# The two attention passes of a vision tower: a new order of score units, a running ring of banks, and folded tiles

## The chip, the cores and the metric

The kernel runs on one core of a Trainium2 chip. The metric is device time in microseconds for one launch, lower is better. Trace times are microseconds from the start of the profiled execution.

## The reference, cut to what matters

64 images become 197 tokens of 192 channels each (a patch embedding, plus a class token). Then attention with 12 heads of 16 channels, in which every operand is fake-quantised to 8 bits with ONE scale per whole tensor, and a mixture of experts with a layernorm. What matters here:

```python
q, k, v = (qkv[0], qkv[1], qkv[2])
attn = jnp.einsum('bhnd,bhmd->bhnm', fake_quant(q), fake_quant(k)) * scale
attn = jax.nn.softmax(attn, axis=-1)
out = jnp.einsum('bhnm,bhmd->bhnd', fake_quant(attn), fake_quant(v))
out = jnp.einsum('bnc,oc->bno', fake_quant(out), fake_quant(w_proj)) + b_proj
```

The scale of `attn` is the maximum over all images and heads, so the softmax has to be known in whole before it can be quantised: the scores are made twice.

## The kernel before, in words

Images are worked in couples, 32 of them. **The first pass** (`attend_maxima`, from L687) makes, for each couple, the integer q and k (two matmuls per group of 4 heads, three groups, into `pqk`; DVE multiplies and rounds into `qkv_y`, L962; POOL takes the magic number off into `qk_int`, L754), the integer v (two full tiles, a tile with tokens 128 to 191 of both images, a tile with the last five tokens), and all scores. SP copies k from the odd rows of `qk_int` to `k_int` (four DMAs, L727, once all three groups are integers) and saves q, k and v to HBM.

The scores of a couple are 37 tiles of 128 partitions x 197: 24 with tokens 0 to 127, 12 with tokens 128 to 191 of both images folded on 128 partitions, and one with the last five tokens of all heads and both images. They are worked in 10 **units**: u0 to u5 are 4 whole tiles each, u6 and u7 are 4 folded tiles each, u8 is 2 folded tiles, u9 is 2 folded tiles and the last tile (the last tile is six matmuls over `q_ends`, L896, each with 128 columns of weights, one after the other in the same accumulation). A unit goes through four engines: PE makes the scores into one of three PSUM tiles `s0..s2` (L881, L889), DVE takes each row's maximum (L976, L970), POOL multiplies it by minus alpha (L810, L808), and ACT makes exp(alpha*s - alpha*max) tile by tile with the row's sum accumulated (L939). PE may use a PSUM tile again when ACT is through with the unit that had it. The order within a couple is u0 to u9; the PSUM tile is u mod 3, but u9 has tile 1:

```python
def bank_of(u):
    return 1 if u == UNITS - 1 else u % 3
def before(u):
    return (6, 9, 8, 0, 1, 2, 3, 4, 5, 7)[u]
```

So u9 waits for the exps of u7, and u1 of the next couple for those of u9. Between the units each engine does a share of the next couple's q, k, v: POOL's copies of token ends after u0, integers after u2, u3 and u4 (`integers`), `q_ends` and the first value tiles after u5, the second value tile after u7 (`values_second`, L787: four instructions whose two scalars are columns in SBUF, all 128 partitions each, with a mask for the image), the last after u9 (`values_last`). All engines run their programs in order; `need_apart` is a wait and a small increment on the same engine.

**Between the passes** (`attend`, from L992) the shifts log(sum)/alpha - max are split into three bfloat16 parts: DVE does the columns of the whole tiles (L1107 to L1111), POOL those of the folded tiles and of the last tile (L1053 to L1062), for the first 4 couples and then for the 28 others. In between them POOL runs `partition_all_reduce` (L1066) for the smallest sum. PE transposes the parts, DVE and ACT copy them out, and DMAs lay them into rows of q in HBM, which k meets with ones.

**The second pass** (`attend`, second half) reloads q, k, v from HBM by SP, makes the scores transposed with the shift in them, in the same units and the same order, with three PSUM tiles `st0..st2`. ACT makes the exps of a whole unit at once (L1320) into one of three SBUF tiles `exps` (`bank_of` again). DVE (units 0, 2, 4, 6, 8, 9) or POOL (1, 3, 5, 7) rounds to bfloat16 integers (L1171). After the scores of u5 PE makes the products of the couple before: 60 matmuls of 198 columns (L1276, L1285). DVE takes them out (`outputs`, L1340, L1341: two instructions for each image's channels 0 to 127 and two for each image's channels 128 to 191, the latter on 64 partitions) and takes each couple's peaks (L1349) after u9. SP's order is q, k and v of one couple, then of the next.

## Time and profile before

| | us |
|---|---|
| median of 3 runs | 2516.96 (2514.52 to 2522.5) |
| the profiled execution | 2516.79 |
| its span, first to last instruction | 2515.0 |
| start of the span to 503 (embedding, norm, scales) | 503 |
| first pass, 503 to 1119 | 616 |
| between the passes, 1119 to 1150 | 31 |
| second pass, 1150 to 1490 | 340 |
| the rest (projection, gate, experts, norm) | 1025 |

How to read it: the busy share of an engine over the whole span says little, since the stages differ. The attention passes repeat one couple 32 times, so that a microsecond in a couple's period is 32 us in the end. "idle ... <-" in a row is the time in which the engine stood still just before, and who released it. PE, DVE, ACT and POOL are TensorE, VectorE, ScalarE and GpSimd, PEld is TensorE's weight load, SPq is the queue on which SyncE issues DMAs.

### The profile page before, as it was taken

What the parts mean: (1) busy time and instruction counts of PE and PEld (TensorE: products, weight loads), DVE (VectorE), ACT (ScalarE), POOL (GpSimd) and SP (SyncE); (2) the same over time, 40 slices, a digit from 0 to 9 for tenths busy, and PEclk for the clock granted to TensorE, in tenths of its full rate; (3) what the DMA queues carried; (4) which work ended last, traced back from release to release, by engine and by line L of the source; (5) the groups of instructions that cost most, each with busy time, mean ns of one, the idle gap of its engine ahead of it and who ended that gap; (6) DMA issues with size and microseconds to landing.
All of it is one profiled execution on the core that took longest, in us unless ns stands there. A gap on an engine that the chain in (4) does not pass through costs nothing. (4 is left out here: it accounts for less than half of the span.)

```text
span 2515.0 us, 51890 instructions
## 1 busy us (share of the span) xinstructions
PE 1568.9 (62%) x12385; PEld 1067.6 (42%) x12386; DVE 1549.1 (62%) x4019; ACT 1298.6 (52%) x3763; POOL 1260.0 (50%) x1953
## 2 busy tenths in 40 slices
PE   2999938645555555534666636666614788876464
PEld 2999934311111111112334323433304667665453
DVE  0555569956666666653666657777746555553797
ACT  0222215358888888875777743333312444443454
POOL 2333300066666666643333323776754566655588
PEclk9999968955555555555666555555557998998787
DMA  5344200011112112114333333333313333332675
GB/s 169 152 164 181 117 30 1 1 61 71 67 61 72 67 60 72 67 42 101 112 107 105 105 100 105 126 124 118 108 59 87 107 101 105 107 106 58 198 244 179
DMA packets 180866, 252.50 MB, mean 100 GB/s; under 512 B 27664, under 2 KB 143839, under 8 KB 177092
## 3 DMA queue, kind: packets, MB, share of 16 engines
q1 hardware_dynamic: 132196, 189.10, 23.9%
q0 software_dynamic: 20704, 40.98, 4.7%
q10 hardware_dynamic: 27888, 21.50, 2.7%
q8 instruction: 34, 0.56, 0.1%
q14 instruction: 44, 0.36, 0.0%
HBM read 140.66 MB, written 107.86 MB: 99 GB/s over the span
## 5 line engine op out<-in xcount | busy, mean ns | idle before, releaser
L939 ACT ACTIVATE exps_summed<-s,neg_shift 128x197 f32<-128x197 f32 x1184 | 484.9, 449 | 118.5 <-POOL neg_shift L810 115.7
L976 DVE TENSOR_REDUCE score_max<-s 128x788 f32 (+3 forms) x320 | 279.9, 891 | 89.5 <-PE s L881 61.8
L2032 POOL DMA_INDIRECT expert_sums<-y_tile,row_places x216 | 215.6, 998 | 165.5 <-ACT y_tile L2132 98.2
L1320 ACT ACTIVATE exps<-st,scalars 128x788 f32<-128x788 f32 (+1 forms) x320 | 256.6, 867 | 71.9 <-DVE probs L1171 30.0
L939 ACT ACTIVATION_READ_ACCUMULATOR exps_summed<-s,neg_shift (+1 forms) x1184 | 270.9, 229 | 0.0
L351 PE MATMUL mm<-w_tok,x_transposed 128*112 128x192 f32 x1344 | 238.7, 328 | 0.0
L351 PEld LDWEIGHTS mm<-w_tok,x_transposed 128*112 128x112 f32 x1344 | 214.5, 178 | 0.1
L1171 POOL TENSOR_SCALAR probs<-exps 128x788 bf16<-128x788 f32 x128 | 108.9, 851 | 197.0 <-ACT exps L1320 196.3
L296 ACT COPY x_transposed<-tp 128x672 f32<-128x672 f32 x112 | 80.6, 719 | 240.9 <-PE tp L342 240.9
L328 POOL TENSOR_SCALAR x_patches<-x_tile 112x768 f32<-112x768 f32 x112 | 93.1, 832 | 223.3 <-PE tp L342 181.7
L1171 DVE TENSOR_SCALAR probs<-exps 128x788 bf16<-128x788 f32 (+1 forms) x192 | 115.3, 614 | 117.8 <-ACT exps L1320 114.0
L889 PE MATMUL s<-k_int,qk_int 16*64 16x197 bf16 x768 | 59.6, 369 | 177.7 <-ACT exps_summed L939 177.7
L881 PE MATMUL s<-k_int,qk_int 16*128 16x197 bf16 x768 | 97.7, 355 | 110.3 <-ACT exps_summed L939 106.2
L382 DVE TENSOR_TENSOR h_rows_all<-mm,posb 112x192 f32<-112x192 f32 (+1 forms) x112 | 40.1, 358 | 178.3 <-PE mm L351 125.7
L962 DVE TENSOR_SCALAR qkv_y<-pqk,scalars 128x394 f32<-128x394 f32 (+1 forms) x192 | 116.9, 609 | 33.9 <-PE pqk L857 20.3
L1560 POOL DMA_INDIRECT listed_rows<-z_rows_a,row_index x99 | 101.4, 1024 | 70.1 <-issue 36.3
L754 POOL TENSOR_SCALAR qk_int<-qkv_y,scalars 128x394 bf16<-128x394 f32 x96 | 122.5, 1276 | 17.4 <-DVE qkv_y L962 10.1
L2125 ACT ACTIVATE g<-dn,down_bias 128x256 f32<-128x256 f32 x216 | 93.1, 494 | 70.6 <-remote 43.3
L810 POOL TENSOR_TENSOR neg_shift<-score_max,neg_alpha 128x4 f32<-128x4 f32 (+1 forms) x320 | 64.0, 200 | 119.6 <-DVE score_max L976 119.4
L2266 PE MATMUL weighted<-sum_a,weight_diagonals 128*128 128x192 f32 (+1 forms) x198 | 65.8, 423 | 84.7 <-DVE weight_diagonals L2322 60.1
L2089 PE MATMUL up<-up_hi,g_hi 128*128 x432 | 112.1, 260 | 7.7 <-issue 4.2
L2158 DVE TENSOR_TENSOR z_lo<-zt,z_hi 128x256 f16<-128x256 f32 x108 | 45.2, 419 | 116.4 <-ACT z_hi L2118 90.8
(411 smaller groups left out, 4714.1 us busy)
## 6 DMA issues: line engine op xcount, KB each, us to landing
x_tile<-in_x SPq DMA_DIRECT2D x24, 1568.0 KB
z_tile<-listed_rows SPq DMA_DIRECT2D x108, 196.0 KB
v_ints<-v_slots SPq DMA_DIRECT2D x32, 480.0 KB, 2.5
v_slots_in<-v_ints SPq DMA_DIRECT2D x32, 480.0 KB, 3.3
q_ints<-qk_int SPq DMA_DIRECT2D x32, 295.5 KB, 2.5
k_ints<-k_int SPq DMA_DIRECT2D x32, 295.5 KB, 2.4
q_shifted<-q_ints SPq DMA_DIRECT2D x32, 295.5 KB, 2.8
k_ones<-k_ints SPq DMA_DIRECT2D x32, 295.5 KB, 3.1
```

What stands on the lines that cost most here:

```text
L328: pool.tensor_scalar(xs[:, w % 2, :].rearrange("p (f w) -> p f w", w=PATCH), src, 1.0, 0.0, ALU.mult, ALU.add).then_inc(xs_ready, 1)
L351: last = nc.tensor.matmul(mm[w % 2][0:ROWS, 0:D], xt[:, w % 2, k * ROWS:(k + 1) * ROWS], w_tok[:, k, :], start=(k == 0), stop=(k == KCH - 1))
L754: pool.tensor_scalar(qk[:, s, g], y[:, g % 2], p.col(C_MQ), None, ALU.subtract).then_inc(used, 1)
L881: ins = nc.tensor.matmul(o[:, 2 * b + m, 0:SEQ], qk[lo:lo + HD, s, g, m * SEQ:m * SEQ + 128], kk[lo:lo + HD, s, g, m * SEQ:(m + 1) * SEQ], ...
L939: act.activation(gone[:, u % 2, k], ps[bank_of(u)][:, k, 0:SEQ], ACT.Exp, scale=alpha, bias=nb[:, s, at:at + 1], accum_out=p.lsum[:, bass. ...
L962: dve.tensor_scalar(y[0:rows, f % 2, 0:w], pqk[0:rows, f % 2, 0:w], p.col(C_CQK if f < GRP else C_CV, 0, rows), p.col(C_MQ, 0, rows), ALU. ...
L976: dve.tensor_reduce(columns(m, u), src, op=ALU.max, axis=AXL.X).then_inc(max_done, 1)
L1171: eng.tensor_scalar(pr[:, s, counted(u):counted(u + 1), 0:SEQ], ex[:, bank_of(u), 0:w], 1.0, 128.0, ALU.mult, ALU.add).then_inc(sem, 1)
L1320: act.activation(ex[:, bank_of(u), 0:w], src, ACT.Exp, scale=alpha, bias=p.col(C_LNSA)).then_inc(e_ready, 1)
L1560: pool.indirect_dma_start(p.zs[:, :], bass.IndirectOffsetOnAxis(ap=idx[0:rows, s, 4 * a + t:4 * a + t + 1], axis=0), z[0:rows, s, t, :], N ...
L2032: pool.indirect_dma_start(p.yD[:, :], bass.IndirectOffsetOnAxis(ap=to[:, k, t:t + 1].bitcast(U32), axis=0), y[:, k, t, :], None, bounds_ch ...
L2089: last = nc.tensor.matmul(pu[b][:, t, 0:D], v[:, k % G, m, rows], w[:, cols], start=first, stop=(m == 1 and w is p.ul))
```

## The change

1. In both passes a unit's place w in the couple is told from its number u. First pass order: 0, 1, 2, 6, 9, 7, 3, 8, 4, 5; second pass order: 0, 1, 2, 3, 6, 7, 8, 9, 4, 5.
2. PSUM tiles are a ring that runs on through two couples (20 units): tile v mod 3, with v the unit's place among the 20. Since 20 is not a multiple of 3, the ring starts anew at every second couple: the first unit there takes the tile of the last but one unit before. The second pass has four `exps` tiles (v mod 4), the first pass still two throw-away outputs.
3. The last tile: each image's ends stand on 64 partitions of their own, so its six matmuls have 64 columns of weights, in three pairs that go to different halves of the array. `values_second` writes 64 partitions per image and needs no mask: its scalars are constants; it waits for its own completions (`used` counts 7 per couple).
4. First pass: POOL's integers go to places 2, 3, 5, its `q_ends` to 6, the first value tiles to 7, the second to 8, the last stays at 9; PE's matmuls for the next couple go to places 0, 1, 2, 5, 6, 8 and DVE's rounding to 1, 2, 3, 6, 7, 9.
5. Between the passes DVE does all the splitting and POOL the reduction alone, and the smallest sum is taken first. SP issues 8 DMAs of the last tile's rows and ACT 16 instead of 12.
6. Second pass: products after place 3; POOL rounds places 1, 3, 5, 7, 8; channels 128 to 191 of both images of a couple stand on 128 partitions of `channels_t1`, taken out by two DVE instructions instead of four; SP moves the odd image's half to its place by one DMA per couple (`unfold`), 32 in all; peaks are taken two couples late, after place 1.

```diff
+ROUND = 2 * UNITS
+LAST_UNIT = UNITS - 1
-STAMP = 138
+STAMP = 69
+ORDER_MAX = (0, 1, 2, 6, 9, 7, 3, 8, 4, 5)
+ORDER_OUT = (0, 1, 2, 3, 6, 7, 8, 9, 4, 5)
-def bank_of(u):
-    return 1 if u == UNITS - 1 else u % 3
-def before(u):
-    return (6, 9, 8, 0, 1, 2, 3, 4, 5, 7)[u]
+def earlier(i, v, slots):
+    back = [x for x in range(v - 1, v - 1 - ROUND, -1) if (x % ROUND) % slots == v % slots][0]
+    return (i, back) if back >= 0 else (i - 1, back + ROUND)
...
                 def values_second(n, s):
                     need_apart(pool, y_ready, 6 * n + 5, tick_p)
                     for m in range(2):
+                        half = slice(64 * m, 64 * m + 64)
+                        need_apart(pool, used, 7 * n + 4 + m, tick_p)
                         for a in range(2):
-                            ins = pool.tensor_scalar(dst, src, p.col(C_MQ), halves[:, m:m + 1], ALU.subtract, ALU.mult)
-                    ins.then_inc(used, 1)
+                            ins = pool.tensor_scalar(dst, src, -MAGIC, 1.0, ALU.add, ALU.mult)
+                        ins.then_inc(used, 1)
+                    need_apart(pool, used, 7 * n + 6, tick_p)
...
-                            if u == 0:
+                            if w == 0:
                                 copies(n + 1, 1 - s)
-                            if u in (2, 3, 4):
-                                integers(n + 1, 1 - s, i + s, u - 2)
-                            if u == 5:
+                            if w in (2, 3, 5):
+                                integers(n + 1, 1 - s, i + s, (2, 3, 5).index(w))
+                            if w == 6:
                                 stamps(n + 1, 1 - s)
+                            if w == 7:
                                 values_first(n + 1, 1 - s, i + s)
-                            if u == 7:
+                            if w == 8:
                                 values_second(n + 1, 1 - s)
...
-                def scores(n, s, u):
-                    need(pe, exp_done, TILES * (n - 1 if u < 3 else n) + counted(before(u) + 1))
-                    o = ps[bank_of(u)]
+                def scores(i, s, w):
+                    n, v, u = 2 * i + s, UNITS * s + w, ORDER_MAX[w]
+                    j, x = earlier(i, v, 3)
+                    need(pe, exp_done, 2 * TILES * j + tiles_before(ORDER_MAX, x + 1))
+                    o = ps[v % 3]
...
-                        for m in range(2):
-                            for g in range(GRP):
-                                ins = nc.tensor.matmul(o[:, 0, 0:SEQ], lq[:, s, m, 128 * g:128 * g + 128],
+                        for g in range(GRP):
+                            for m in range(2):
+                                ins = nc.tensor.matmul(o[64 * m:64 * m + 64, 0, 0:SEQ], lq[:, s, m, 64 * g:64 * g + 64],
...
-            POOL_UNITS = (1, 3, 5, 7)
-            DVE_UNITS = (0, 2, 4, 6, 8, 9)
+            ON_POOL = (1, 3, 5, 7, 8)
-            ex = p.sb("exps", [128, 3, 4, SEQ], F32, c)
+            ex = p.sb("exps", [128, 4, 4, SEQ], F32, c)
...
+                    def unfold(n):
+                        sp.wait_ge(o_out, 3 * n + 3)
+                        sp.dma_start(p.o1[0:D1, bass.ds((2 * n + 1) * SEQ, SEQ)],
+                                     p.o1[D1:128, bass.ds(2 * n * SEQ, SEQ)]).then_inc(apart, 16)
                     with sp.Fori(2, COUPLES // 2) as i:
                         load(i, 0)
+                        unfold(2 * i - 3)
                         load(i, 1)
+                        unfold(2 * i - 2)
...
                                 scores(i, s, w)
-                                if u == 5 and not (isinstance(n, int) and n == 0):
+                                if w == 3 and not (isinstance(n, int) and n == 0):
                                     products(n - 1, 1 - s, i - 1 + s)
```

## Rows read from the trace of the kernel before

**Rows 1.** The page's slices of the whole span: granted TensorE clock in tenths

```profile
PEclk9999968955555555555666555555557998998787
```

**Rows 2.** Busy time by stretch; columns PE, PEld, DVE, ACT, POOL, clock, DMA share, GB/s

```profile
560.00:1080.00 520.00, 273.76 (x1892) 95.49 (x1890) 331.15 (x473) 434.61 (x2060) 331.50 (x802) 0.50 0.18 67
1180.00:1460.00 280.00, 188.86 (x3092) 108.07 (x3092) 180.49 (x438) 219.75 (x275) 110.00 (x166) 0.61 0.34 108
```

**Rows 3.** First pass, groups of instructions: page row, the line's own row, then by form

```profile
L939 ACT ACTIVATE exps_summed<-s,neg_shift 128x197 f32<-128x197 f32 x1184 | 484.9, 449 | 118.5 <-POOL neg_shift L810 115.7
...
L939 ACT ACTIVATE exps_summed<-s,neg_shift x1184: 415/429/621, 523.2 to 1118.2; 128x197 f32<-128x197 f32 x198
...
L976 DVE TENSOR_REDUCE score_max<-s 128x788 f32 x224 | 215.5, 972 | 62.6 <-PE s L881 52.5 <-PE s L889 10.1
L754 POOL TENSOR_SCALAR qk_int<-qkv_y,scalars 128x394 bf16<-128x394 f32 x96 | 122.5, 1276 | 17.4 <-DVE qkv_y L962 10.1 <-issue 6.8
...
L787 POOL TENSOR_SCALAR v_slots<-qkv_y,scalars,image_rows 128x96 bf16<-128x96 f32 x128 | 86.5, 686 | 1.0
...
L777 POOL TENSOR_SCALAR v_slots<-qkv_y 128x192 bf16<-128x192 f32 x64 | 21.5, 351 | 0.0
```

**Rows 4.** Timeline, one whole unit of the first pass: start, duration

```profile
802.07 0.51 PE L881 MATMUL s<-k_int,qk_int 16*128 16x197 bf16 x4 [2.64 <-ACT exps_summed L939]
...
802.74 0.98 DVE L976 TENSOR_REDUCE score_max<-s 128x788 f32 x1 [1.89 <-PE s L881]
...
803.98 0.21 POOL L810 TENSOR_TENSOR neg_shift<-score_max,neg_alpha 128x4 f32<-128x4 f32 x1 [0.72 <-DVE score_max L976]
...
804.32 0.43 ACT L939 ACTIVATE exps_summed<-s,neg_shift 128x197 f32<-128x197 f32 x1
```

**Rows 5.** Timeline, the last unit of the same couple

```profile
816.25 0.38 PE L889 MATMUL s<-k_int,qk_int 16*64 16x197 bf16 x4 [2.37 <-ACT exps_summed L939]
...
816.56 1.17 PE L896 MATMUL s<-k_int,q_ends 128*128 128x197 bf16 x6
...
817.88 0.36 DVE L970 TENSOR_REDUCE score_max<-s 128x197 f32 x1 [3.39 <-PE s L896]
...
819.44 0.43 ACT L939 ACTIVATE exps_summed<-s,neg_shift 128x197 f32<-128x197 f32 x1 [1.96 <-POOL neg_shift L810]
```

**Rows 6.** Timeline, from the third group of integers to the copied keys

```profile
809.46 1.27 POOL L754 TENSOR_SCALAR qk_int<-qkv_y,scalars 128x394 bf16<-128x394 f32 x1
...
810.76 2.42 SPq L727 DMA_DIRECT2D k_int<-qk_int  x4
...
814.65 0.34 SPq L731 DMA_DIRECT2D k_ints<-k_int  x1
```

**Rows 7.** Timeline, between the passes

```profile
1129.30 0.86 DVE L1108 TENSOR_TENSOR shift_rest<-shift,shift_parts 128x672 f32<-128x672 f32 x1
...
1132.29 0.38 POOL L1066 PARTITION_ALL_REDUCE scalars<-scalars  x1 [6.53 <-issue]
...
1140.45 0.89 POOL L1055 TENSOR_TENSOR shift_rest<-shift,shift_parts 128x336 f32<-128x336 f32 x1 [6.88 <-issue]
```

**Rows 8.** Second pass: the exps' own row, then a timeline of one couple

```profile
L1320 ACT ACTIVATE exps<-st,scalars x320: 591/911/961, 1154.6 to 1479.8; 128x788 f32<-128x788 f32 x128, 128x394 f32<-128x394 f32 x32
...
1306.00 3.43 ACT L1320 ACTIVATE exps<-st,scalars 128x591 f32<-128x591 f32 x4 [1.18 <-PE st L1255]
...
1309.93 1.84 PE L1276 MATMUL po_images<-probs,v_slots_in 128*32 128x198 bf16 x40
1310.42 2.54 ACT L1320 ACTIVATE exps<-st,scalars 128x788 f32<-128x788 f32 x3 [0.99 <-DVE probs L1171]
...
1312.53 0.87 PE L1247 MATMUL st<-q_shifted,k_ones 32*64 32x197 bf16 x20
...
1313.22 2.21 ACT L1320 ACTIVATE exps<-st,scalars 128x788 f32<-128x788 f32 x3 [0.26 <-PE st L1247]
```

**Rows 9.** Busy time in the stretch after the products; columns as rows 2

```profile
1312.50:1316.00 3.50, 1.89 (x38) 1.04 (x34) 1.93 (x5) 2.67 (x4) 1.71 (x3) 0.84 0.43 140
```

More of the change, by code:

```diff
@@ L983, in body @@
                         n = 2 * i + s
-                        for u in range(UNITS):
-                            maxima(n, u)
-                            if u in (1, 2, 3, 4, 6, 8) and not (last and s == 1):
-                                rounded(n + 1, (1, 2, 3, 4, 6, 8).index(u))
+                        for w in range(UNITS):
+                            maxima(i, s, w)
+                            if w in (1, 2, 3, 6, 7, 9) and not (last and s == 1):
+                                rounded(n + 1, (1, 2, 3, 6, 7, 9).index(w))
                 repeat(dve, COUPLES // 2, body)
@@ L1021, in attend @@
             pt = [p.ps(f"shift_t{j}", [PARTS, 8, 128], BF16, c) for j in range(4)]
-            chain, chain_p, red, lnd, base, first, second, turn, out_a, out_v = p.sems(
-                c, "d", "chain chain_p red lnd base first second turn out_a out_v")
+            chain, low, red, lnd, split, turn, out_a, out_v = p.sems(c, "d", "chain low red lnd split turn out_a out_v")
             at_first = p.sems(c, "d", "at_first_sp at_first_act")
@@ L1220, in body @@
                             for u in range(UNITS):
-                                if u in POOL_UNITS:
-                                    rounding(pool, p_pool, tick_p, n, s, u)
-                                if u == 8 and not (last and s == 1):
+                                if u in ON_POOL:
+                                    rounding(pool, p_pool, tick_p, i, s, u)
+                                if u == 6 and not (last and s == 1):
                                     stamps(n + 1, 1 - s, i + s)
@@ L1230, in _, with scores @@
                 def _(pe):
-                    def scores(n, s, u):
-                        need(pe, e_ready, UNITS * (n - 1 if u < 3 else n) + before(u) + 1)
-                        o = ps[bank_of(u)]
+                    def scores(i, s, w):
+                        n, v, u = 2 * i + s, UNITS * s + w, ORDER_OUT[w]
+                        j, x = earlier(i, v, 3)
+                        need(pe, e_ready, ROUND * j + x + 1)
+                        o = ps[v % 3]
                         if u < 6:
```

353 lines of the change are left out of this document (173 added, 180 removed).

## The prediction

> **What bounds the kernel now.** I read the stretches first. Outside the attention passes (1,528 us) nothing is touched, so the answer lies in 503 to 1490. In [rows 2] the first pass has ACT busy 435 of 520 us, POOL and DVE about 331, PE 274; the second has ACT 220 of 280, PE 189, DVE 180. The reader should see that ACT leads in both and is full in neither. The ACT row [rows 3] gives the first pass's length: 1,184 exps from 523.2 to 1118.6, or 595.4 / 32 = 18.6 us a couple. Its page row has 118.5 us of idle, 115.7 of it released by POOL's negated maxima. Four exps of 0.40 us pitch make a whole unit (ACT's unit from 804.32 [rows 4] holds 1.6 us), so 37 make 14.8 us: that is the floor, and 3.8 us a couple are stalls or broken cadence. The second pass, from the exps' own row [rows 8], runs from 1154.6 to 1480.5: 325.9 / 32 = 10.2 us. Its exps take 3.43 + 2.54 + 2.21 = 8.2 us; 2.0 us are stalls.
>
> **Why it stalls.** A PSUM tile is held from its matmuls to its exps. [Rows 4]: matmuls at 802.07, maxima at 802.74, minus alpha at 803.98, exps at 804.32, i.e. 2.25 us of latency. With the hand-over to PE (I take 0.17 us from the nominal end of the exps; a choice, as the last accumulator read hangs over) a unit needs 2.4 us of other exps to cover it. Two whole units give 3.2. The last unit [rows 5] needs 819.44 - 816.25 = 3.2 us, and since it waits for u7, only u8's two tiles (0.8 us) cover it. That is where ACT stood 1.96 us, and smaller gaps before u0, u1, u4 and u8 make up the rest.
>
> **First pass, part by part.** *Last tile.* Six serial matmuls took 1.17 us [rows 5]; in pairs on separate halves, three rounds, I take 0.6: the latency falls to about 2.7. *Order.* Cover of each place = the tiles of the two before it: u9 has u2 and u6, 3.2 us, enough; u7 and u3 have 2.8; u4 and u5 at places 8 and 9 have 2.4, just enough. *Values_second.* Four instructions of 0.686 [rows 3] become four of 96 elements with constants; the row with constants and 192 elements is 0.351. I take 0.28, plus three waits for own completions at 0.2: 1.7 instead of 2.7 us on POOL. Bounds: 1.2 and 3.3.
> Going through a couple by hand with these, DVE 0.97 per maximum and 0.5 to 0.7 per rounding behind it, POOL 1.28 for each group of integers [rows 3]: places 0 to 8 hold ACT's cadence with slack 0 to 0.8 us; place 9 is late by 0.2 (values_second in front of its negation), and the next couple's place 0 by 0.2 (the last values, which now wait for a rounding after place 9). Sum 14.8 + 0.4 = 15.2 us.
> At every second couple the ring starts anew: place 0 then has one unit of cover, 1.6 against 2.4, a stall of 0.8; it takes the 0.2 above into itself, and DVE, which must take the next maxima bunched, and POOL with its integers add 0.3 at place 3 and 0.4 at place 4. About 16.3 us. Mean 15.75; I take 15.9 for what a hand schedule leaves out. Ends: 15.2 (no seam cost) and 17.0 (each of five places with no slack loses 0.25).
> *The copied keys.* The integers end 1.27 us after 809.46, and the k_int copies are there at 814.65 [rows 6]: 3.9 us, of which 2.4 is issue on SP. They are moved from place 4 to place 5 of a shorter couple. By the hand schedule they land 0.5 us after PE could start the next couple, still 0.4 before POOL is ready for it. So I charge 0, with 0.5 as the other end. Also moved past SP's queue: nothing, as v's DMA still follows the last values.
> First pass: (18.6 - 15.9) x 32 = **86 us** (51 to 109). The start waits for the same key copies; 0.
>
> **Between the passes** (36 us from the last exps to the first). POOL idled 6.53 us before the reduction and 6.88 before its next tensor_tensor [rows 7]; PE's transposes waited for POOL's share of the splitting behind both, some 4.8 us more. The Trainium skill, GPSIMD Engine Reference, section on instruction dispatch, says that the first call of a freshly loaded kernel pays about 6 us; by that figure the two gaps would be 12 us and not 13.4. After the change DVE does 15 instructions for 4 couples (an estimate of 0.2 to 0.3 each, a third to a quarter of the 0.86 for 672 elements [rows 7]: 3.4 us, from 1123.0), then about 1 us of scale work, and for 28 couples STT 1.3 plus three triples of casts (about 1.05) and two of subtractions (0.86 [rows 7] + 0.5 + 0.25): 6.4. They end at about 1136.6, 8.5 us earlier. The reduction's load starts with the block and is hidden. The load back is not gone: it now stands before the first `k_ends` of the second pass, after two memsets, 6.9 us from there. POOL's first rounding is then due some 9.5 us into the pass, where ACT can run five units without it; I charge 1.7. SP's 20 DMAs here (8 of them new) at 0.4 to 0.6 us each [rows 6] end by 1136 to 1140, before the pass can start; ACT's 4 more by 1135. Net **7 us** (bounds 2 and 8.5).
>
> **Second pass.** The scores-to-exps latency of a unit is some 0.6 us, so the order matters less. Two stalls go: the 1.18 before u9 [rows 8], whose cover is now 0.85 + 0.51 against 1.3, and the 0.99 before u3 for an `exps` tile that DVE rounds behind outputs and peaks: with four tiles and peaks elsewhere that wait has 2.5 us of cover. But PE is late next. In [rows 8] the products start at 1309.93, the next scores at 1312.53, their exps at 1313.22: 3.3 us, plus 0.5 for the scores in front. ACT has 2.54 us of queued exps there, before and after the change alike, so 1.3 to 1.45 us of stall stays where the products run at 1.2 GHz. It was half hidden behind the u3 stall. Whether they do: the clock was 0.61 on the mean [rows 2], 0.84 in the stretch behind the products [rows 9], where PE had been busy without a gap, and back to 0.5 before the next ones. PE's work at the low clock is about 8.5 us, so it will be busy nearly throughout at that clock, and rises should come oftener and reach the products in some couples; at 2.4 GHz they take half and the stall is gone. I take half of the couples: 8.25 + 0.1 + 0.7 = 9.05 us. Ends: 8.25 and 9.75. (10.2 - 9.05) x 32 = **36 us** (14 to 62).
> Costed at nothing: outputs save two of eight DVE instructions a couple (DVE has slack, 180 of 280); `unfold` waits on SP in front of the next loads, but for outputs a couple old by then, and the loads have a couple's time; POOL's fifth rounding takes it to about 4.9 of 9 us. The end: one more couple of peaks (+0.9), outputs -0.5, the last unfold beside the reduction: 0.
>
> **Sum.** Against the profiled execution, 2516.8 (span 2515.0 and 1.8 around it; the median of the runs is 0.2 higher): 2516.8 - 86 - 7 - 36 = **2388 us**.
>
> **Rivals.**
> *A. The products bind all of the second pass* (TensorE stays at 1.2 GHz there). For it: PEclk 5 and 6 in those slices [rows 1], and a tighter loop with faster matmuls has more PE idle, which brings the clock down. Against: [rows 9]. Period 9.7: saving 16 instead of 36, 2408 us.
> *B. The first pass finds a second bound*, POOL or the keys: places 8, 9 and 0 have no slack and POOL holds 9 instructions there. For: POOL is at 331 of 520 now [rows 2], that is 12 us per couple against 15.9. Against: 1 us of it goes. Period 17.0: saves 51, total 2423.
> *C. All goes as drawn up:* the clock rises and the seam is absorbed: 15.4 and 8.4 us; 102 + 8 + 58: 2349.
> *D. Slower: the keys.* PE starts no couple before the k_int copies. Each microsecond by which they land after the slack is a microsecond per couple, 32 in all. The rest brings about 43 us and the first pass 2.7 per couple, so it decides at 3.9 + 0.5 + 2.7 + 1.3 = 8.4 us from integers to keys, against 3.9 in [rows 6]. SP issues only these and three more DMAs per couple. At 9 us: 2536.
> *E. It does not do what it says:* the stalls come from the four-engine latency whatever the order; they move to the places with 2.4 us of cover. Then 18.3 us and an unchanged second pass: 2500.
>
> **How the numbers follow.** The forecast (2375 to 2400) 0.42, A 0.2, B 0.17, C 0.13, E 0.03, D 0.03, no gain by several parts at once 0.02. 8 in 10 reach from below C's 2349 to 2436, past B. A measurement can tell 0.3% (7.5 us). Faster 0.94, same 0.02, slower 0.04.
>
> **What would show it.** ACT's period in the first pass 15 to 16.5 us, alternating by 1 us from couple to couple, its longest idle at the first unit of every second couple; the gap at u9 gone; L787 at 0.3 us; exps of the second pass starting about 29 us after the last of the first, with a POOL gap of 6.9 us before its first `k_ends`; second-pass periods of two kinds, 8.3 and 9.7. Wrong if PE waits for `k_int` in each couple, if ACT's releaser stays POOL for over 2 us a couple, or if DVE turns up as ACT's releaser in the second pass.

## The result, and the profile after

The median fell from 2517.86 to 2402.3 us (four runs each, 2399.47 to 2406.86 after), a ratio of 0.9542 with a 95% interval of 0.952 to 0.9563. The profiled execution took 2401.83 us, its span 2400.1. Forecast: 2388, between 2346 and 2436. One execution in experiment 4 took 6372.06 us, the other three 2402.89 to 2405.01; it counts in no comparison.

The stages, cut at the first and last exps of each pass and at the first matmul of the projection, in us. The last two lines are the kernel before profiled once more later (run 8), and the difference of after and before:

| | to the first exps | pass 1 | between | pass 2 | turn | rest | span |
|---|---|---|---|---|---|---|---|
| before | 523.2 | 595.0 | 36.4 | 325.2 | 34.4 | 1000.8 | 2515.0 |
| after | 521.5 | 507.5 | 26.3 | 300.8 | 34.6 | 1009.4 | 2400.1 |
| before again | 525.6 | 594.7 | 36.2 | 325.4 | 34.2 | 1010.7 | 2526.8 |
| after - before | -1.7 | -87.5 | -10.1 | -24.4 | +0.2 | +8.6 | -114.9 |

The passes of the kernel before repeat within 0.3 us in these two traces. In all runs a first pass that an edit leaves alone stays within 0.9 us of its value here, a second pass within 2.0. So the experiments below are read by their passes, each against the same pass of after.

The +8.6 of the rest is an effect of the change, though its code is the same there but for one operand's slice. It lies in the projection, norm and gate. From the first to the last `h_rows_out`, which DVE makes from the projection, it is 303.4 us before and 312.8 after:

```profile
L1792 DVE SCALAR_TENSOR_TENSOR h_rows_out<-proj,scalars,h_rows_in x99: 401/409/419, 1515.7 to 1819.1; 128x192 f32<-128x192 f32 x98, 64x192 f32<-64x192 f32 x1
  issue: 2.7, 6
...
L1806 DVE SCALAR_TENSOR_TENSOR h_rows_out<-proj,scalars,h_rows_in x99: 399/409/419, 1392.2 to 1705.0; 128x192 f32<-128x192 f32 x98, 64x192 f32<-64x192 f32 x1
  issue: 18.1, 10
...
1488.39 1.07 DVE L1806 SCALAR_TENSOR_TENSOR h_rows_out<-proj,scalars,h_rows_in 128x192 f32<-128x192 f32 x3 [3.28 <-issue]
```

It is 303.4 to 303.5 us in the four traces made from the kernel before (before, runs 5, 8 and 12) and 312.3 to 315.8 in the ten made from after. At four places in after DVE stands 3.1 to 3.3 us, where the profile shows nothing that it waits for ("issue"). Why, no run shows. What lies behind the last `h_rows_out` is 695.9 and 695.1 us here; it is that part which drifts, to 705.7 in the kernel before profiled again.

From the page of the kernel after (clock slices in tenths; then line, engine, operation, tiles | busy us, mean ns | idle before, releaser):

```profile
PEclk9999987965555555556556555555558999887777
L964 ACT ACTIVATE exps_summed<-s,neg_shift 128x197 f32<-128x197 f32 x1184 | 482.7, 478 | 39.8 <-POOL neg_shift L831 38.5
L1336 ACT ACTIVATE exps<-st,scalars 128x788 f32<-128x788 f32 (+1 forms) x320 | 246.6, 882 | 57.8 <-PE st L1268 46.0
```

L964 answers to L939 in [rows 3]: the exps cost what they did, and their idle time went from 118.5 to 39.8 us. L1336 answers to L1320 in [rows 8]: now it is PE, with the scores of the folded units (L1268), that ACT waits for. The two lines by themselves (min/median/max ns, first and last start):

```profile
L964 ACT ACTIVATE exps_summed<-s,neg_shift x1184: 415/450/767, 521.5 to 1029.0; 128x197 f32<-128x197 f32 x198
...
L1336 ACT ACTIVATE exps<-st,scalars x320: 582/918/977, 1055.3 to 1356.1; 128x788 f32<-128x788 f32 x128, 128x394 f32<-128x394 f32 x32
```

Busy time by stretch, columns as in [rows 2], first pass and second pass:

```profile
560.00:1040.00 480.00, 273.83 (x1977) 84.15 (x1977) 362.52 (x520) 455.45 (x2188) 298.32 (x840) 0.50 0.21 76
1100.00:1340.00 240.00, 172.44 (x2968) 99.41 (x2968) 132.35 (x341) 200.60 (x262) 120.37 (x182) 0.59 0.40 125
```

ACT is now busy 95% of the first pass, against 84% in [rows 2], and 84% of the second, against 78%. (The stretches are parts of the passes.)

Timeline of the kernel after, places 8 and 9 of a couple and the start of the next (start, duration, engine, and the idle time before in brackets):

```profile
803.45 0.20 POOL L831 TENSOR_TENSOR neg_shift<-score_max,neg_alpha 128x4 f32<-128x4 f32 x1 [0.74 <-DVE score_max L1001]
...
803.81 0.50 POOL L806 TENSOR_SCALAR v_slots<-qkv_y 64x96 bf16<-64x96 f32 x2 [0.16 <-issue]
...
804.50 0.51 POOL L806 TENSOR_SCALAR v_slots<-qkv_y 64x96 bf16<-64x96 f32 x2 [0.19 <-POOL v_slots L806]
...
805.42 0.20 POOL L831 TENSOR_TENSOR neg_shift<-score_max,neg_alpha 128x4 f32<-128x4 f32 x1 [0.42 <-POOL v_slots L806]
...
805.76 0.43 ACT L964 ACTIVATE exps_summed<-s,neg_shift 128x197 f32<-128x197 f32 x1 [0.22 <-POOL neg_shift L831]
...
807.87 0.43 ACT L964 ACTIVATE exps_summed<-s,neg_shift 128x197 f32<-128x197 f32 x1 [0.37 <-POOL neg_shift L831]
```

The whole of `values_second` lies between two negations, 803.65 to 805.42, and ACT idles 0.22 us ahead of place 9 and 0.37 ahead of the next couple's place 0, where the ring starts anew. POOL is the releaser, as drawn up. PE does wait for copied keys at 9 of the couples, 0.9 us at most (7.5 in all), but the periods of ACT with such a wait are as long as those without.

Between the passes and at the start of the second:

```profile
1031.81 1.39 DVE L1099 TENSOR_REDUCE scalars<-exp_sum 128x1 f32<-128x1184 f32 x1 [4.37 <-PEq L232]
...
1037.67 0.38 POOL L1069 PARTITION_ALL_REDUCE scalars<-scalars  x1 [9.96 <-issue]
...
1045.65 0.16 DVE L1118 CAST last_parts<-shift_rest 128x28 bf16<-128x28 f32 x1
...
1050.90 0.79 POOL L1224 MEMSET k_ends<- 128x828 bf16 x1 [12.85 <-POOLq L1052]
...
1054.76 0.85 PE L1260 MATMUL st<-q_shifted,k_ones 32*128 32x197 bf16 x12 [5.52 <-DMA k_ones<-k_ints]
...
1063.88 0.53 POOL L1232 TENSOR_TENSOR k_ends<-k_ones,k_rows 128x60 bf16<-128x60 bf16 x2 [12.08 <-issue]
...
1065.34 2.85 ACT L1336 ACTIVATE exps<-st,scalars 128x788 f32<-128x788 f32 x4 [5.88 <-POOL probs L1179]
```

DVE ends its splitting 16.8 us behind the last exps (forecast 18.0), but POOL stood 12.08 us in front of the first `k_ends` and not the 6.9 forecast from [rows 7], and ACT stood 5.88 us for it. Not all of such a gap is the loading of POOL's code. The 9.96 us ahead of the reduction begin with POOL's last instruction of the first pass; DVE's first instruction of this stage comes at 1031.81, and from there it is 5.9 us. The 12.08 hold the wait for the first keys, which `k_ends` reads and which PE has at 1054.76, 3.0 us after POOL's memsets; from there it is 9.1 us, and 7.1 to 9.3 in the eight traces with this gap.

SP's queue and PE, ahead of couple 3 of the second pass (counted from 0):

```profile
1073.46 12.40 SPq L1038 DMA_DIRECT2D q_ints<-shift_last  x24
```

```profile
1089.73 0.84 PE L1260 MATMUL st<-q_shifted,k_ones 32*128 32x197 bf16 x12 [4.28 <-DMA k_ones<-k_ints]
```

SP issues the last tile's shift rows, 24 DMAs for couples 4 to 31, 0.52 us each, ahead of a couple's load; PE stands 4.28 us for its keys, and from the last tile of couple 2 to that of couple 3 it is 12.18 us instead of 9.27. The change doubled their number, from 12. The kernel before, same view:

```profile
1169.79 5.34 SPq L1013 DMA_DIRECT2D q_ints<-shift_last  x12
```

A steady couple of the second pass, PE and ACT:

```profile
1202.37 1.84 PE L1296 MATMUL po_images<-probs,v_slots_in 128*32 128x198 bf16 x40
1203.97 1.06 PE L1305 MATMUL po_rest<-probs,v_slots_in 128*32 128x198 bf16 x20
1204.97 0.72 PE L1268 MATMUL st<-q_shifted,k_ones 32*64 32x197 bf16 x20
1205.67 7.71 ACT L1336 ACTIVATE exps<-st,scalars 128x788 f32<-128x788 f32 x10 [1.56 <-PE st L1268]
```

Ten units of exps now run without a gap, 7.71 us, and then ACT waits 1.24 to 1.57 us for the scores behind the products. The period is 9.2 to 9.3 us. All 1,280 of the first products lie within 322 to 373 ns with a median of 370, as in the kernel before:

```profile
L1296 PE MATMUL po_images<-probs,v_slots_in x1280: 322/370/373, 1070.3 to 1359.8; 128*32 128x198 bf16 x183
```

Of the 640 products of L1305, which close the block, 12 took 249 to 266 ns: the last four in three of the 32 couples. So TensorE's clock does rise, but behind the block or at its very end, and not in every couple. In the couple after the one shown, the products run from 1211.63 to 1213.9 at 1.2 GHz, their last four behind that at 249 to 259 ns, and the stretch that follows them has 1.00, 2.4 GHz (columns as before):

```profile
1214.00:1216.00 2.00, 0.96 (x36) 0.55 (x30) 0.31 (x1) 1.37 (x2) 0.41 (x1) 1.00 0.28 52
```

### The profile page after: what moved, and what is told of

It reads as the page before. It is cut to its first block and busy times, and to the rows that moved or that the text cites. A ratio compares the mean times of both kernels' runs of the same rounds, so it can differ in the third digit from the quotient of the medians.

```text
span 2400.1 us, 52305 instructions
## 1 busy us (share of the span) xinstructions
PE 1553.8 (65%) x12385; PEld 1054.0 (44%) x12386; DVE 1517.3 (63%) x3943; ACT 1280.4 (53%) x3763; POOL 1228.5 (51%) x1967
## 5 line engine op out<-in xcount | busy, mean ns | idle before, releaser
L964 ACT ACTIVATE exps_summed<-s,neg_shift 128x197 f32<-128x197 f32 x1184 | 482.7, 478 | 39.8 <-POOL neg_shift L831 38.5
L1001 DVE TENSOR_REDUCE score_max<-s 128x788 f32 (+2 forms) x320 | 284.7, 894 | 107.6 <-PE s L905 95.5
L964 ACT ACTIVATION_READ_ACCUMULATOR exps_summed<-s,neg_shift (+1 forms) x1184 | 304.4, 260 | 0.0
L2046 POOL DMA_INDIRECT expert_sums<-y_tile,row_places x216 | 220.7, 1022 | 150.7 <-ACT y_tile L2146 102.7
L1336 ACT ACTIVATE exps<-st,scalars 128x788 f32<-128x788 f32 (+1 forms) x320 | 246.6, 882 | 57.8 <-PE st L1268 46.0
L1179 POOL TENSOR_SCALAR probs<-exps 128x788 bf16<-128x788 f32 (+1 forms) x160 | 129.9, 819 | 141.0 <-ACT exps L1336 118.0
L1179 DVE TENSOR_SCALAR probs<-exps 128x788 bf16<-128x788 f32 (+1 forms) x160 | 96.2, 601 | 146.6 <-ACT exps L1336 144.7
L986 DVE TENSOR_SCALAR qkv_y<-pqk,scalars 128x394 f32<-128x394 f32 (+1 forms) x192 | 116.7, 608 | 24.4 <-POOL qk_int L770 21.2
L905 PEld LDWEIGHTS s<-k_int,qk_int 16*128 16x128 bf16 x768 | 26.0, 106 | 224.6 <-ACT exps_summed L964 214.9
L1260 PE MATMUL st<-q_shifted,k_ones 32*128 32x197 bf16 x768 | 81.7, 333 | 57.8 <-ACT exps L1336 45.2
```

What stands on the lines that cost most here:

```text
L905: ins = nc.tensor.matmul(o[:, 2 * b + m, 0:SEQ], qk[lo:lo + HD, s, g, m * SEQ:m * SEQ + 128], kk[lo:lo + HD, s, g, m * SEQ:(m + 1) * SEQ], ...
L964: act.activation(gone[:, v % 2, k], ps[v % 3][:, k, 0:SEQ], ACT.Exp, scale=alpha, bias=nb[:, s, to:to + 1], accum_out=p.lsum[:, bass.ds(n ...
L986: dve.tensor_scalar(y[:, f % 2, 0:w], pqk[:, f % 2, 0:w], p.col(C_CQK if f < GRP else C_CV), p.col(C_MQ), ALU.mult, ALU.add).then_inc(y_re ...
L1001: dve.tensor_reduce(columns(m, u), src, op=ALU.max, axis=AXL.X).then_inc(max_done, 1)
L1179: eng.tensor_scalar(pr[:, s, at(u):at(u) + size(u), 0:SEQ], ex[:, v % 4, 0:size(u)], 1.0, 128.0, ALU.mult, ALU.add).then_inc(sem, 1)
L1336: act.activation(ex[:, v % 4, 0:size(u)], src, ACT.Exp, scale=alpha, bias=p.col(C_LNSA)).then_inc(e_ready, 1)
```

## The experiments

The theory after the result: the first pass gains by order, ring and lighter POOL work together, in shares unknown; the second is bound by products at 1.2 GHz in one block, plus two stalls that come once. The rival for the first pass: the order is nearly all of it. For the second: it is DVE, or the number of `exps` tiles.

**1. The old order of units, all else as after.**

```diff
-ORDER_MAX = (0, 1, 2, 6, 9, 7, 3, 8, 4, 5)
+ORDER_MAX = (0, 1, 2, 3, 4, 5, 6, 7, 8, 9)
```

> The changed kernel, but with the first pass's units in the order 0 to 9; the running ring, the folded last tile and all else stay. If cover is what counts (a unit needs about 2.4 us of other exps between its predecessor in the PSUM tile and itself, u9 about 2.9): u9 has u7 and u8 before it, 2.4 us, and the next u0 has u8 and u9, 2.0 us, so 0.5 + 0.4 us a couple are lost, the first pass goes from 15.9 to 16.8 us a couple and the time to about 2431 us. If the first pass gained by lighter work on POOL and PE and not by the order: 2402 within 5 us.

Median 2411.84 us (the kernel before beside it 2516.1), ratio 0.9579 (0.9555 to 0.9603). First pass 518.8 us, 11.3 more than after; the exps' idle on the page:

```profile
L964 ACT ACTIVATE exps_summed<-s,neg_shift 128x197 f32<-128x197 f32 x1184 | 482.9, 483 | 52.1 <-POOL neg_shift L831 51.8
```

The result lies between the two expectations (2431, or 2402 within 5). The order that gives the change its name is worth 0.35 us a couple, an eighth of the first pass's gain, where cover alone was to make it 0.9. The other 76 us belong to the other parts.

**2. POOL's load brought forward.** A tiny tensor_tensor on POOL, of the kind that the second pass begins with, right behind the reduction.

```diff
                     pool.partition_all_reduce(p.col(C_LMIN), p.col(C_TMP), 128, RMAX).then_inc(red, 1)
+                    pool.tensor_tensor(idle[:], p.idf[:, 0:4], p.idf[:, 4:8], ALU.add)
```

> The changed kernel with one small tensor_tensor on POOL (128 x 4, into a tile nobody reads) right behind the reduction between the passes. If the 12.1 us before POOL's first k_ends are the loading of code, which then happens in POOL's idle time between the passes: the gap goes, the 5.9 us for which ACT stood at the start of the second pass go with it, and the time falls by 5 to 6 us to about 2397. If the gap is something else (the arrival of k, say): no change, 2402.

Median 2403.06 us, ratio 0.9548 (0.9521 to 0.9576): no change by the median. Second pass 297.3 us, only 3.5 less. Timeline of this run:

```profile
1046.52 0.47 POOL L1071 TENSOR_TENSOR idle_sum<-ident_f 128x4 f32<-128x4 f32 x1 [7.01 <-issue]
...
1056.00 0.53 POOL L1234 TENSOR_TENSOR k_ends<-k_ones,k_rows 128x60 bf16<-128x60 bf16 x2 [2.72 <-DMA k_ones<-k_ints]
...
1056.52 10.92 ACT L1338 ACTIVATE exps<-st,scalars 128x788 f32<-128x788 f32 x14 [2.39 <-PE st L1262]
...
1069.41 0.78 SPq L1197 DMA_DIRECT2D k_ones<-k_ints  x1
...
1071.59 11.98 SPq L1038 DMA_DIRECT2D q_ints<-shift_last  x24
...
1076.72 0.84 PE L1262 MATMUL st<-q_shifted,k_ones 32*128 32x197 bf16 x12 [5.22 <-DMA k_ones<-k_ints]
...
1087.44 0.84 PE L1262 MATMUL st<-q_shifted,k_ones 32*128 32x197 bf16 x12 [2.92 <-DMA k_ones<-k_ints]
```

The load now takes 7.01 us, where POOL has nothing to do, and the stall of 5.88 is gone; `k_ends` waits 2.72 us for its keys alone. But the pass now reaches the loads sooner. PE waits 5.22 us for the keys of couple 2, which after did not: SP issues them at 1069.41, behind the rows of the whole tiles and ahead of the 24 DMAs, and they are there 7.2 us later. Then it waits 2.92 us for those of couple 3, behind the 24. The two couples are late (13.08 and 11.04 us). Of 5.9 us, 2.4 are taken back.

**3. Products in three parts**, an image after place 2, the other after place 4, the channels 128 to 191 after place 9.

```diff
-                                if w == 3 and not (isinstance(n, int) and n == 0):
-                                    products(n - 1, 1 - s, i - 1 + s)
+                                if w in (2, 4, 9) and not (isinstance(n, int) and n == 0):
+                                    products(n - 1, 1 - s, i - 1 + s, ((2, 4, 9).index(w),))
```

> The changed kernel with the 60 products of the second pass in three parts, after places 2, 4 and 9, instead of in one block after place 3. If the block is what ACT waits for (1.3 to 1.5 us of idle per couple ahead of place 4): each part takes some 0.9 us, ACT's queued exps cover it, and the second pass goes from 9.2 to about 8.2 us a couple: some 30 us less, 2372. If PE's throughput at 1.2 GHz is the bound however the work is cut: under 6 us less, 2396 or more.

Median 2385.47 us, ratio 0.9474 (0.9451 to 0.9498). Second pass 285.7 us, 15.1 less than after, with a steady period of 8.60 us: between the two expectations (30 less, or under 6). Two things stand in the rows: PE's first part now waits for DVE's taking out of the couple before, which the whole block had not met, and PE waits 8.25 us for the keys of couple 3.

```profile
1202.39 1.02 PE L1297 MATMUL po_images<-probs,v_slots_in 128*32 128x198 bf16 x20 [0.94 <-DVE channels_t L1357]
```

```profile
1080.78 12.25 SPq L1038 DMA_DIRECT2D q_ints<-shift_last  x24
```

Counted from the pass's first exps the 24 DMAs start 2.4 us later than in after (20.6 and 18.2), since on SP they stand behind a load of v that waits for products, and these now end at place 9. So the block of products is what made ACT wait, and its length is not the whole of PE's work: at the same 1.2 GHz (clock 0.50 from 1090 to 1300) the pass is shorter.

**4. The load of couple 3 among the 24 DMAs**, behind the first six.

```diff
                     for a in range(4):
+                        if a == 1:
+                            load(1, 1)
                         for k in range(3):
...
-                    load(1, 1)
```

> The changed kernel with the loads of couple 3 issued on SP before three quarters of the 24 last-tile DMAs and not behind them. In the changed kernel PE waited 4.3 us for k of couple 3. If SP's 12.4 us of issuing is the cause: 2.5 to 4 us less, about 2399. If the transfers themselves are slow there: no change, or slower by the placements coming late for couple 4.

Median 2403.19 us, ratio 0.9549 (0.9517 to 0.958). Second pass 298.0, 2.8 less than after: the first periods (from last tile to last tile) are 10.32, 8.93, 9.26 and 10.58 us, where after has 10.22, 9.27, 12.18 and 9.27. The excess of 2.9 us is gone, but 1.3 of it comes back in the next couple, whose keys now stand behind the other 18 DMAs (PE waits 2.56 us). Some 0.8 of the 2.8 us lies ahead of all this, in the first couple, where POOL's gap happens to be 11.19 and not 12.08. By the median nothing can be told.

**5. The kernel before with the running ring alone** (first pass).

```diff
-                    need(pe, exp_done, TILES * (n - 1 if u < 3 else n) + counted(before(u) + 1))
-                    o = ps[bank_of(u)]
+                    j, x = earlier(i, v, 3)
+                    need(pe, exp_done, TILES * (2 * j + x // UNITS) + counted(x % UNITS + 1))
+                    o = ps[v % 3]
```

> The kernel before with one thing of the change: in the first pass the PSUM tile of a unit is its place among the 20 units of two couples mod 3. Order, last tile, POOL's work and everything else are as before. u9 then waits for the exps of u6 and not of u7 (2.4 us of cover instead of 0.8), the next u0 for those of u7. If the ring is what the first pass gained by: its 595 us fall by 45 to 65, to 530 to 550, and the time to 2455 to 2475. If the order or the lighter work is needed for it: by under 25 us, 2490 or more.

Median 2467.91 us against 2529.81, ratio 0.9764 (0.9747 to 0.978). First pass 534.5 us, as the first expectation had it: 60 of the 87.5 us, from the tile numbers alone. (The ring was added to the kernel before; it was not taken out of after.) The exps' idle:

```profile
L946 ACT ACTIVATE exps_summed<-s,neg_shift 128x197 f32<-128x197 f32 x1184 | 484.2, 476 | 63.2 <-POOL neg_shift L815 63.1
```

In the kernel before, u9 had tile 1 and waited for u7, with u8's two tiles for cover, and u1 of the next couple waited for u9. In the ring, u9 waits for u6, and only every second couple starts anew.

**6. After, with the masked values_second** (128 partitions, scalars from columns).

```diff
-                            ins = pool.tensor_scalar(dst, src, -MAGIC, 1.0, ALU.add, ALU.mult)
+                            ins = pool.tensor_scalar(dst, src, p.col(C_MQ), halves[:, m:m + 1], ALU.subtract, ALU.mult)
```

> The changed kernel with POOL's four instructions of the second value tile in their old form (128 partitions, scalars in columns, a mask; 0.69 us each and not 0.25), at their new place and with their new waits. If POOL has no slack at places 8 and 9, as forecast: 1.0 to 1.7 us more per couple, the first pass goes from 507 to 540 to 560 us and the time to 2435 to 2455. If ACT's cadence has slack for it: under 10 us more.

Median 2467.37 us, ratio 0.9754 (0.9738 to 0.977). First pass 560.5 us, 53 more than after and 26 more than run 5. The same place of a couple:

```profile
802.61 1.37 POOL L807 TENSOR_SCALAR v_slots<-qkv_y,scalars,image_rows 128x96 bf16<-128x96 f32 x2 [0.19 <-issue]
804.19 1.35 POOL L807 TENSOR_SCALAR v_slots<-qkv_y,scalars,image_rows 128x96 bf16<-128x96 f32 x2 [0.21 <-POOL v_slots L807]
805.96 0.21 POOL L832 TENSOR_TENSOR neg_shift<-score_max,neg_alpha 128x4 f32<-128x4 f32 x1 [0.42 <-POOL v_slots L807]
...
806.29 0.43 ACT L965 ACTIVATE exps_summed<-s,neg_shift 128x197 f32<-128x197 f32 x1 [1.98 <-POOL neg_shift L832]
```

From the first value instruction to the next negation it is 3.35 us here and 1.61 in after; the difference of 1.74 us, 32 times, is 55.7, and the pass grew by 53, the upper end of what was expected. Here a microsecond of POOL is a microsecond of the pass.

**7. Runs 2 and 3 together, with two mends:** each part of the products waits only for the outputs that it overwrites, and SP issues q and k of couple 2, the 24 DMAs, then v of couple 2 and couple 3.

```diff
-                            need(pe, o_out, 3 * n)
+                        need(pe, o_out, 3 * n - 2 + parts[-1])
...
-                    load(1, 0)
+                    load_qk(1, 0)
...
+                    load_v(1, 0)
                     load(1, 1)
```

> The changed kernel with the products in three parts after places 2, 4 and 9, each part now waiting only for the output that frees its own PSUM columns (the split run had PE idle 0.9 us a couple for the last output); the early tensor_tensor between the passes; and on SP the last-tile DMAs issued between couple 2's q and k and its v, so that v's wait does not hold them up. If these three are separate costs: the second pass has 32 couples of 8.2 us and no gap over 2 us in its first five: 268 us instead of 301, and the time is 2370. If DMA at the start of the second pass is the bound once the code load is out of the way: 276 us or more, 2378 or more.

Median 2378.8 us against 2529.81, ratio 0.9403 (0.9385 to 0.942): better than the change (0.9542), the intervals don't meet. Second pass 265.4 us. Page row, and busy time in the steady part:

```profile
L1347 ACT ACTIVATE exps<-st,scalars 128x788 f32<-128x788 f32 (+1 forms) x320 | 250.2, 875 | 18.7 <-PE st L1270 11.9
```

```profile
1090.00:1300.00 210.00, 188.04 (x2936) 89.91 (x2936) 131.18 (x335) 200.51 (x256) 119.13 (x181) 0.50 0.48 144
```

ACT is busy 200.5 of 210 us, PE 188, at a granted clock of 0.50 throughout. So at 1.2 GHz the second pass comes within 5% of ACT's own length, with a steady period of 8.1 us. Two single stalls are left: PE waits 4.71 us for the keys of couple 2 and 2.73 for those of couple 3. The pass is shorter than expected (268), the whole is longer (2370), but the kernel before beside it is 12 us longer too.

**8. The kernel before once more**, to tell drift in the rest from an effect.

> The kernel before, unchanged, for a second trace. In the trace of the changed kernel the part behind the attention passes, which no edit touches, is 8.6 us longer than in that of the kernel before (1009.4 and 1000.8 us), and 1011 to 1014 in four others. If that is drift of the chip or from trace to trace: 1005 to 1012 here. If the change does something to that part: within 3 us of 1000.8.

2528.52 us against 2529.81; its stages are in the table above. The rest took 1010.7 us, close to after's 1009.4, but for another reason: up to the last `h_rows_out` it is as long as before, and the drift lies behind it. The total of the stage hides what the change does to it.

**9. The last tile's matmuls not in pairs** (image by image, 64 columns each, in both passes).

```diff
-                        for g in range(GRP):
-                            for m in range(2):
+                        for m in range(2):
+                            for g in range(GRP):
```

> The changed kernel with the six matmuls of the last tile image by image and not in pairs of images, in both passes, so that matmuls behind one another use the same half of the array (5 rounds of 0.17 us instead of 3). If the pairing carries some of the gain: the first pass goes up by 5 us or more from its 507.5. If u9 has slack at its new place: both passes stay within 2 us (507.5 and 300.8).

One execution: 2406.01 us. First pass 508.4, second 300.3: 0.9 more and 0.5 less than after, no more than they differ between traces. In the new order, where the last unit has two whole units of cover, the pairs bring nothing that can be told.

**10. Old order and masked values**, both edits of runs 1 and 6.

> The changed kernel with both the masked form of the second value tile on POOL and the plain order 0 to 9 in the first pass. The masked form alone made the first pass 560.5 us, the plain order alone 518.8. If the masked form hurts because POOL's own load is too much at the end of a couple, whatever the order: about 572 (the two losses add). If it hurts because the new order has put whole units, whose maxima wait for nothing, where POOL is held: 535 to 545, less than in the new order.

One execution: 2460.7 us. First pass 554.4, less than the 560.5 of the new order with the same masked values. Neither expectation came (572, or 535 to 545): the masked form costs 36 us in the old order and 53 in the new, which fits neither reason alone. With POOL heavy, the new order is a loss of 6 us; with POOL light, a gain of 11.3.

**11. Three `exps` tiles in the second pass.**

```diff
-            ex = p.sb("exps", [128, 4, 4, SEQ], F32, c)
+            ex = p.sb("exps", [128, 3, 4, SEQ], F32, c)
```

> The changed kernel with three tiles for the second pass's exps instead of four (ring of three, as PSUM has). If the fourth tile took away the wait for DVE's rounding: the second pass goes from 300.8 to 320 or more. If moving the peaks to place 1 and rounding ahead of the outputs did that, and the products hide the rest: 300 to 306.

One execution: 2416.87 us. Second pass 305.7, 4.9 more than after. ACT's groups from 1090 to 1330, this run's:

```profile
L1336 ACT ACTIVATE exps<-st,scalars 128x788 f32<-128x788 f32 (+1 forms) x253 | 199.2, 870 | 41.8 <-PE st L1268 33.1 <-POOL probs L1179 8.5
```

The fourth tile takes away a wait of 8.5 us for POOL's rounding. The wait for DVE's that stood in [rows 8] is gone with three tiles too.

**12. The kernel before with the ring and the light values_second**, order, places and last tile as before.

```diff
+                        half = slice(64 * m, 64 * m + 64)
+                        need_apart(pool, used, 7 * n + 4 + m, tick_p)
...
-                            ins = pool.tensor_scalar(dst, src, p.col(C_MQ), halves[:, m:m + 1], ALU.subtract, ALU.mult)
+                            ins = pool.tensor_scalar(dst, src, -MAGIC, 1.0, ALU.add, ALU.mult)
+                        ins.then_inc(used, 1)
+                    need_apart(pool, used, 7 * n + 6, tick_p)
```

> The kernel before with two parts of the change in the first pass: the running ring of banks, and values_second with constants on 64 partitions per image (with its waits). Order of units, POOL's and DVE's places, the six serial matmuls of the last tile, and the second pass stay as before. The ring alone gave a first pass of 534.5 us here, all parts with the old order 518.8, all parts 507.5. If the ring and the light values are nearly the whole of the gain wherever POOL's work stands, the first pass takes 508 to 522 us, and what is left for the new order with its new places is at most 12 us. If the light form only pays where POOL's instructions have been moved back to back (places 8 and 9), as in the two runs with masked values, it is worth little in the old places: 530 to 534 us. Second pass 325, between 36 in either case.

Median 2359.6 us against 2420.15 for the kernel before, ratio 0.9759 (0.9727 to 0.9791), the ratio of run 5. (Both kernels are some 100 us shorter here. In this run it is the rest: 903.6 us against 1010.7, and the difference lies behind the last `h_rows_out`; the kernel before was not traced beside it.) First pass 533.2 us, 1.3 less than run 5; second pass 327.2. The second expectation holds: in the old places the light form is worth nothing.

```profile
L949 ACT ACTIVATE exps_summed<-s,neg_shift 128x197 f32<-128x197 f32 x1184 | 483.5, 484 | 64.0 <-POOL neg_shift L818 62.5
```

The first pass of all variants, in us:

| | masked values_second | light values_second |
|---|---|---|
| before | 595.0 | not run |
| before with the ring | 534.5 | 533.2 |
| after's places, old order | 554.4 | 518.8 |
| after's places and order | 560.5 | 507.5 |

## Why the prediction was right, and where it was not

**The total** came out 14 us above the forecast and inside the range, close to rival A's 2408. By parts: first pass 87.5 for 86, between the passes 10.1 for 8.5 ahead of the late rounding, second pass 24.4 for 36 with 1.7 more charged to its start. The rest is 8.6 us longer, a term that the prediction put at nothing with "Outside the attention passes (1,528 us) nothing is touched": its code was not, but DVE stands 18.1 us and not 2.7 in front of `h_rows_out` there. The stretch before the first exps, 1.7 us shorter, gives some of it back. With 11.6 us missing in the second pass, the total is near the forecast partly because the range was wide enough for both.

**First pass.** The period went from 18.6 to 15.9 us, to the tenth what was forecast, and by the mechanism that was drawn up. The periods alternate between 16.14 and 15.84, but the wait at the seam (where the ring starts anew) falls before the first exps of its couple and so into the period before; the 0.3 is not the seam's cost. Counted unit by unit, from one exps' start to the next beyond the 0.40 us pitch, ACT is late by 0.36 us at place 9 of each couple and by 0.20 at place 0 without a seam, where 0.2 and 0.2 were forecast. The seam adds 0.28 at place 0, 0.29 at place 1 and 0.33 at places 3 and 4 together: 0.9 for the 1.1 of the sum. Place 8 loses 0.05 to 0.16, the others nothing. That is 16.0 us in the steady couples, for 15.75 by hand; the first and the last are shorter (14.9 and 15.1), and the 0.15 "for what a hand schedule leaves out" covered the rest. The prediction never priced the parts one by one. Read as "cover of each place", it credited the order; the runs credit the ring, added first, with 60 us. The explanation of the stall was right ([rows 5]: u9 waits for u7 with 0.8 us of cover), but it is the tile's number that mends it, and the old order with a ring has nearly the cover of the new. Values_second was counted as 1 us less POOL work; its worth is none in the old places and 1.7 us a couple in the new ones. The forecast is thus right for the whole and would have been wrong for any half of the change: new places without the light values are 20 us worse than old places (554.4 against 534.5).

Between run 12 (533.2) and run 1 (518.8) lie the new places of POOL, PE and DVE and the paired last tile in the old order. These 14 us were not divided: run 9 clears the pairs only in the new order.

**Rival B and D.** POOL is the second bound when it is heavy, in run 6 with a period of 17.5 us, which is B's mechanism; the light values keep it away. PE's waits for copied keys, 7.5 us in all, lengthened no couple (D).

**Between the passes.** Right in kind, with DVE's splitting done 1.2 us sooner than estimated. The Trainium skill, GPSIMD Engine Reference, section on instruction dispatch, puts the first call of a freshly loaded kernel at about 6 us; in this case it was 7.01 us in run 2 and 5.9 ahead of the reduction in after, near it, and up to 9.1 at the start of the second pass, which is more. The step that failed is "after two memsets, 6.9 us from there": it left out the wait of `k_ends` for its keys, 3.0 us here, and the load itself was 2.2 us longer than the 6.9. That changes 1.7 us of late rounding into 5.88.

**Second pass.** Two sizes in the sum were wrong in opposite directions. The step that failed outright is "I take half of the couples" to have products at 2.4 GHz: none had, by the 322 to 373 ns of L1296, and only the last four matmuls of the block in three couples. The clock rose behind the products, as [rows 9] showed, and was back at 0.50 before the next. So the stall was 1.24 to 1.57 us in each couple, as the prediction had it for the low clock, and not 0.7 on the mean. Against that, exps without gaps take 7.71 us a couple and not 8.25: the three pieces of [rows 8], added up, each had an instruction's start and end in it, which a gapless run has once. So the period is 9.2 us, not 9.05, and not A's 9.7. The missing 11.6 us are 0.15 in each couple, 5.88 at the start and 2.9 at couple 3 (13.6), less some 1.5 in the first couple, which has no products. The step that failed at couple 3 is the count of "SP's 20 DMAs here (8 of them new)": it holds for the stretch between the passes, and the 24 for couples 4 to 31 (12 of them new), in the second pass itself, were left out. How much of the wait comes from the doubling was not tried; in the runs made from the kernel before, with 12, PE waited up to 1.65 us, and for the keys of couple 2. A's mechanism bound the pass; run 3 shows it by splitting the block (15.1 us less), and run 7 takes it to within 5% of ACT's own time.

**The fourth `exps` tile** was given 0.99 us of stall to remove, with the moved peaks; run 11 gives the tile 0.15 us a couple of its own. What removed DVE's lateness, the order, the peaks or the units moved to POOL, was not divided.

## What to carry to other kernels

Where tiles are handed round a ring, look first at the one assignment that breaks it: here it was worth 60 us of 87 when added first, more than the order, the lighter instructions, their places and the pairing together behind it. Price the parts of a change in company, since a lighter instruction was worth nothing in the old schedule and 53 us in the new one. Don't count on a higher TensorE clock where the trace shows it rising only behind the block that needs it; splitting the block and placing its parts between the units that the next engine waits for brings the time back at the low clock. And read an untouched stage too, part by part: its code may stay while its time does not.

## What the runs showed of the hardware that was not expected

- The change of POOL's code cost 7.01 us where POOL had nothing else to do (run 2), 5.9 ahead of the reduction counted from the stage's first instruction, and 7.1 to 9.3 us at the start of the second pass counted from the arrival of the keys. It is hidden by an instruction of the new kind issued early (run 2). That the load begins only with the keys, and that the transfers beside it make it longer, was not tried by itself.
- TensorE stayed at 1.2 GHz through 210 us in which it was busy for 188 (run 7), while in after, with 172 of 240, it had 0.59 on the mean. Filling its gaps did not raise the clock here.
- 24 small DMAs in SP's queue took 12.4 us to issue, 0.52 us each, and PE stood 4.3 us for the keys loaded behind them, 8.2 us in run 3 and 2.9 in run 2. Keys issued just ahead of them took 7.2 us from issue to landing in run 2 and 5.4 in after, those of couples 5 to 31 3.1 to 3.4.
- Instructions of 96 elements on POOL took 0.69 us with scalars in columns on 128 partitions, and 0.27 us with constants on 64; which of the two differences does it was not tried.
- DVE stood 18.1 us in front of `h_rows_out` in after and 2.7 in before, at an unchanged instruction and with nothing shown that it waits for; the stretch took 303.4 to 303.5 us in four traces and 312.3 to 315.8 in ten.
- Behind that stretch the same code took about 100 us less in run 12 than in the kernel before (rest 903.6 and 1010.7 us), while the first pass stayed within 0.9 us and the second within 2.0.
